# New order tables: value products before gate products, the last scans on the decays themselves, other keep-warm products

## The reference

```python
# layer 0, b = 16 sequences
x = x + attention(q, k, v of layernorm(x), mask_self) @ w_ao + b_ao
x = x + attention(q of layernorm(x), k, v of ctx, mask_cross) @ w_co + b_co
x = x + gelu(layernorm(x) @ w1 + b1) @ w2 + b2
# attention: softmax(q k^T / 4 * mask - 10000 (1 - mask)) v, 16 heads of 16
# layer 1, time mix (states start from ctx)
xn = ln(x); sx = shift(xn) - xn
m = tanh((xn + sx*maa_x) @ maa_w1) -> 5 low-rank mixes @ maa_w2
xw, xk, xv, xr, xg = xn + sx * (stack_i + m_i)
w = exp(-exp(time_decay + tanh(xw @ decay_w1) @ decay_w2))
r, k, v, g = xr@Wr, xk@Wk, xv@Wv, silu(xg@Wg)
s[t+1] = w[t]*s[t] + k[t] v[t]        # a scan along the 128 tokens
o[t] = r[t] . (s[t] + u k[t] v[t])
x = x + (groupnorm(o) * g) @ Wo
# layer 1, channel mix: x = x + sigmoid(xr@Wr') * (relu(xk@Wk')**2 @ Wv')
```

## Time and profile before

| What | Value |
|---|---|
| median of the timed runs | 695.53 us |
| profiled execution, its own time | 695.38 us |
| its span from first to last instruction | 693.6 us |
| around the span | 1.8 us |
| PE busy | 645.6 us (93%) |
| DVE busy | 597.0 us (86%) |
| ACT busy | 570.5 us (82%) |
| POOL busy | 314.9 us (45%) |
| mean granted TensorE clock | 0.985 |
| rounds in the steady part | 37.2 us each |

### The profile page before, as it was taken

The page is one execution under the profiler, slowest core; times in us unless marked ns, Lnnn a source line. Parts: engine busy times, 40 slices in busy tenths (PEclk is TensorE's granted clock), DMA queues, the critical chain, the costliest instruction groups (busy, mean ns, idle before and its releaser), DMA issues.

```text
span 693.6 us, 17394 instructions
## 1 busy us (share of the span) xinstructions
PE 645.6 (93%) x5923; PEld 564.4 (81%) x5923; DVE 597.0 (86%) x1432; ACT 570.5 (82%) x2075; POOL 314.9 (45%) x440
## 2 busy tenths in 40 slices
PE   6778999999999999999999999999999989898876
PEld 5656888788888898898988888888888878787665
DVE  2577668999999999999999999999999996967672
ACT  2579989899999999999999999999999986763311
POOL 1143353555455463626364645455463634441211
PEclk9999999999999999999999999999999999999997
DMA  8920022231405050504122231405050504020200
GB/s 302 329 69 9 1 78 61 62 78 49 98 8 139 1 147 1 144 3 112 35 77 70 62 86 43 104 2 145 1 146 1 139 8 115 24 70 1 69 8 9
DMA packets 53726, 50.45 MB, mean 73 GB/s; under 512 B 6030, under 2 KB 48902, under 8 KB 53254
## 3 DMA queue, kind: packets, MB, share of 16 engines
q1 hardware_dynamic: 53638, 49.34, 25.6%
HBM read 28.62 MB, written 3.93 MB: 47 GB/s over the span
## 4 chain that ended last, share of the span: by engine, by line
PE 71%; ACT 13%; DVE 8%; issue 5%; POOL 2%; DMA 0%; SPq 0%; POOLq 0%; ACTq 0%; DVEq 0%
PE PS_B L542 13%; PE PS_T L637 7%; PE PS_S L542 7%; PE PS_D L549 5%; PE PS_S L618 5%; PE PS_T L645 4%; PE PS_T L549 4%; PE PS_S L549 3%; ACT HG L1240 3%; PE PS_D L783 2%; ACT SC L1199 2%; ACT L1199 2%; PE PS_B L677 2%; PE PS_B L699 2%; ACT PT L1209 2%
## 5 line engine op out<-in xcount | busy, mean ns | idle before, releaser
L1199 ACT ACTIVATE SC<-SC,NMX 128x128 f32<-128x128 f32 x512 | 199.7, 400 | 5.6 <-DVE NMX L934 5.4
L1199 ACT ACTIVATION_READ_ACCUMULATOR SC<-SC,NMX 128x1 f32 x512 | 102.3, 200 | 0.0
L934 DVE TENSOR_REDUCE NMX<-SC 128x4 f32<-128x512 f32 x128 | 85.8, 673 | 0.9 <-POOL SC L1381 0.8
L637 PE MATMUL PS_T<-CST,SC 128*128 128x128 f32 x512 | 79.7, 279 | 5.7 <-ACT SC L1199 2.8
L1209 ACT ACTIVATE PT<-PS_T 128x512 f32<-128x512 f32 x120 | 70.8, 590 | 7.0 <-PE PS_T L637 6.8
L1015 DVE TENSOR_TENSOR_SCAN SS<-W,AJ 128x1024 f32<-128x1024 f32 x32 | 73.1, 2283 | 0.5 <-ACT AJ L1291 0.4
L637 PEld LDWEIGHTS PS_T<-CST,SC 128*128 128x128 f32 x512 | 60.2, 144 | 14.5 <-ACT PT L1209 5.3
L1379 POOL TENSOR_TENSOR SC<-SC,MADD 128x512 f32<-128x512 f32 x48 | 60.2, 1273 | 12.0 <-DVE SC L909 11.9
L542 PE MATMUL PS_B<-MX,W 128*128 128x128 f32 x512 | 62.9, 276 | 0.7 <-ACT KR L1256 0.7
L1381 POOL TENSOR_TENSOR SC<-SC,MADD 128x512 f32<-128x512 f32 x32 | 40.7, 1273 | 48.3 <-DVE SC L909 48.3
L909 DVE TENSOR_TENSOR SC<-PS_S,MASK 128x512 f32<-128x512 f32 x80 | 52.1, 684 | 11.5 <-PE PS_S L618 11.5
(11 more groups left out here) (208 smaller groups left out, 1602.8 us busy)
## 6 DMA issues: line engine op xcount, KB each, us to landing
W<-EW SPq DMA_DIRECT2D x32, 512.0 KB, 4.7
V<-values_by_head SPq DMA_DIRECT2D x28, 512.0 KB, 5.7
W<-in_weights SPq DMA_DIRECT2D x1, 4160.0 KB, 19.6
ENC<-in_enc SPq DMA_DIRECT2D x16, 128.0 KB, 2.4
out<-X SPq DMA_DIRECT2D x16, 128.0 KB, 6.0
X<-in_x SPq DMA_DIRECT2D x1, 1920.0 KB, 15.8
values_by_head<-VC SPq DMA_DIRECT2D x14, 128.0 KB, 1.8
W<-in_weights SPq DMA_DIRECT2D x1, 1280.0 KB, 8.7
```

Source lines behind the costliest of these rows:

```text
L637: last = pe.transpose(PS_T[:, j * T:(j + 1) * T], SC[:, nr(b, a) % 2, g, j, :], ident)
L934: dve.tensor_reduce(NMX[:, nr(b, a) % 2, GH * g:GH * g + GH], SC[:, nr(b, a) % 2, g], AX_X, ALU.max, negate=True)\
L1199: last = act.activation(SC[:, nr(b, a) % 2, g, j, :], SC[:, nr(b, a) % 2, g, j, :], ACT.Exp, bias=NMX[:, nr(b, a) % 2, h:h + 1], accum_out ...
```

## The change

Four things change. First, the value stream moves from the last mixing step to the first and the gate stream to the last; the value product goes to the second bank of `PS_B`, in front of the key and receptance products and with a release of its own (`b_vps`); the gate product keeps its bank and gets `b_gps`. The low-rank columns are brought into a new order by more, smaller DMAs, and the gate's rows lie in a zeroed tile `MG`. Second, for the last sequence each scan is split into 8 scans of 128 elements that read `EW`, without the DMA into `W8`, and the multiplication by r follows each group directly. Third, in the first four attentions the scaled keys are made by VectorE; the turn of the value biases comes behind the first scores, the old output bias is added by a product with the identity, and ScalarE copies the rows out. Fourth, 27 of the keep-warm products around the end are gone (`b_turn` 3 to 0 and 6 to 1, `d_turn` 5 to 0, `d_keyrec` 14 to 0 for the sequences named), and all five order tables are new.

```diff
-MIX_TURNS = [(1, 4), (0, 3), (2,)]
+MIX_TURNS = [(1, 2), (0, 3), (4,)]
-    ('a_query', 1, 1): 2, ('b_turn', 0, 15): 3, ('b_turn', 1, 15): 6, ('d_out', 0, 14): 2, ('d_turn', 0, 14): 5,
-    ('d_keyrec', 0, 14): 14, ('d_val', 0, 14): 2, ('d_own', 0, 15): 2, ('d_read', 0, 15): 2,
+    ('a_query', 1, 1): 2, ('b_turn', 0, 15): 0, ('b_turn', 1, 15): 1, ('d_out', 0, 14): 2, ('d_turn', 0, 14): 0,
+    ('d_keyrec', 0, 14): 0, ('d_val', 0, 14): 2, ('d_own', 0, 15): 2, ('d_read', 0, 15): 2,
...
+    ("b_mlp2", 1, 3), ("a_pv", 0, 1), ("a_val", 0, 0), ("d_keyrec", 0, 5), ("d_keyrec", 1, 5), ("b_turn", 1, 3),
...
             def b_wspread(b, _):
+                if b == B - 1:
+                    return
...
             def b_low1(b, _):
                 pe.wait_ge(b_xx, b + 1)
+                if not later(b):
+                    pe.wait_ge(in_mw, 128)
...
-                        last = pe.matmul(PS_B[:, 0, m * T:(m + 1) * T], w("maa2", 2, C, m * P, (m + 1) * P), MT[:, 0, :],
+                        last = pe.matmul(PS_B[:, 0, m * T:(m + 1) * T], MG[:, m * P:(m + 1) * P], MT[:, 0, :],
...
             def b_decay2(b, _):
                 pe.wait_ge(b_dt, b + 1)
+                pe.wait_ge(b_v, b + 1)
...
             def b_valgate(b, k):
                 if k:
-                    to_channels(PS_B[:, 0, C:2 * C], "g", C, 0, MX[:, 4]).then_inc(b_vgps, 1)
-                else:
+                    pe.wait_ge(b_mx, 3 * b + 3)
                     pe.wait_ge(b_kr, b + 1)
-                    pe.wait_ge(b_mx, 3 * b + 3)
-                    to_channels(PS_B[:, 0, 0:C], "v", C, 0, MX[:, 2])
+                    to_channels(PS_B[:, 0, C:2 * C], "g", C, 0, MX[:, 4]).then_inc(b_gps, 1)
+                else:
+                    pe.wait_ge(b_mx, 3 * b + 1)
+                    pe.wait_ge(b_mix, 3 * b + 2)
+                    to_channels(PS_B[:, 1, C:2 * C], "v", C, 0, MX[:, 2]).then_inc(b_vps, 1)
...
+            def a_key(b, a):
+                if nr(b, a) < FIRST:
+                    dve.wait_ge(a_kps, nr(b, a) + 1)
+                    for par in range(2):
+                        for t in range(CT):
+                            last = dve.tensor_scalar(KP[:, par, t, :], keys[:, t * T:(t + 1) * T],
+                                                     CST[:, K_PAR + par:K_PAR + par + 1], KB[:, a, par, t:t + 1],
+                                                     ALU.mult, ALU.add)
+                    last.then_inc(a_dk, 1)
...
+                if b == B - 1:
+                    for d in range(RS):
+                        last = dve.tensor_tensor_scan(SS[:, t, d, :], EW[:, t, :], AJ[:, t, d, :], 0.0, ALU.mult, ALU.add)
+                    last.then_inc(d_s, 1)
+                    dve.wait_ge(d_s, 2 * b + t + 1)
+                    r = KR[:, 1, t, :].unsqueeze(1).to_broadcast([P, RS, T])
+                    dve.tensor_tensor(SS[:, t], SS[:, t], r, ALU.mult).then_inc(d_rs, 1)
+                    return
...
+                if not later(b, a) and g == 0 and half == 0:
+                    act.wait_ge(set_bv, 1)
+                    act.activation(BVT[:, :, :, :].rearrange("p k t n -> p (k t n)"), PS_D[:, :], ACT.Copy)\
+                        .then_inc(set_bvt, 1)
+                    act.wait_ge(set_bo, 1)
+                    at = ROWS.index("ao"), ROWS.index("co")
+                    for k in range(2):
+                        last = act.activation(ROW[:, at[k], :], PS_D[:, k * C:(k + 1) * C], ACT.Copy)
+                    last.then_inc(set_rows, 1)
```

More of the change, by code:

```diff
@@ L237, in build @@
         a_k = sem("a_k")
+        a_dk = sem("a_dk")
         a_q = sem("a_q")
@@ L602, in a_query @@
                     to_channels(queries, "qkv", 3 * C, 0, A_LT).then_inc(a_qps, 1)
-                    if not later(b):
-                        pe.wait_ge(in_rows, IN_ROWS)
-                        pe.wait_ge(set_dve, 2)
-                        for k in range(2):
-                            last = turn(PS_D[:, k * C:(k + 1) * C], row(f"bv{k}"))
-                        last.then_inc(set_bv, 1)
             def a_scores(b, a):
@@ L622, in a_scores, with a_prob_turn @@
                 if not later(b, a):
+                    pe.wait_ge(in_rows, IN_ROWS)
+                    pe.wait_ge(set_dve, 2)
+                    for k in range(2):
+                        last = turn(PS_D[:, k * C:(k + 1) * C], row(f"bv{k}"))
+                    last.then_inc(set_bv, 1)
+            def a_prob_turn(b, arg):
+                a, g = arg
+                if not later(b, a) and g == 0:
                     pe.wait_ge(in_wa, IN_WA)
                     pe.wait_ge(set_bvt, 1)
-                    to_tokens(PS_D[:, 0:C], "ao", C, 0, BVT[:, 0])
-                    to_tokens(PS_D[:, C:2 * C], "co", C, 0, BVT[:, 1]).then_inc(set_bo, 1)
-            def a_prob_turn(b, arg):
-                a, g = arg
+                    for k, name in enumerate(("ao", "co")):
+                        for kt in range(CT):
+                            pe.matmul(PS_D[:, k * C:(k + 1) * C], BVT[:, k, kt, :], w(name, kt, C, 0, C),
+                                      start=(kt == 0), stop=False)
+                        last = pe.matmul(PS_D[:, k * C:(k + 1) * C], ident, row(name), start=False, stop=True)
+                    last.then_inc(set_bo, 1)
                 warm("a_prob_turn", arg, b)
@@ L692, in b_low2 @@
                     pe.wait_ge(b_mt, b + 1)
-                    if not later(b):
-                        pe.wait_ge(in_mw, 32)
                     for t in range(CT):
@@ L909, in a_mask @@
                 dve.tensor_tensor(masked, PS_S[:, g], over_heads(mask), ALU.mult).then_inc(a_masked, 1)
-                if not later(b, a) and g == 0:
-                    dve.wait_ge(set_bo, 1)
-                    for k, name in enumerate(("ao", "co")):
-                        last = dve.tensor_tensor(row(name), PS_D[:, k * C:(k + 1) * C], row(name), ALU.add)
-                    last.then_inc(set_rows, 1)
             def a_addmask(b, arg):
@@ L1023, in d_rstate @@
             def d_rstate(b, t):
-                if t == 0 or b >= B - LAST:
+                if t == 0 and b < B - 1 or b == B - 2:
                     dve.wait_ge(d_s, 2 * b + t + 1)
@@ L1177, in a_key @@
                 last.then_inc(a_k, 1)
-                if not later(b, a) and par:
-                    act.wait_ge(set_bv, 1)
-                    act.activation(BVT[:, :, :, :].rearrange("p k t n -> p (k t n)"), PS_D[:, :], ACT.Copy)\
-                        .then_inc(set_bvt, 1)
             def a_lessmask(b, _):
```

138 lines of the change are left out of this document (80 added, 58 removed).

## The result

The changed kernel takes 715.75 us (median of three, 714.64 to 716.05) against 695.53: 2.84% slower, with a ratio of 1.0284 and an interval of 1.027 to 1.0298. I had forecast 692.3. The profiled execution (715.75 us, span 714.0) is split at the start of the scores, the products of queries and keys; there is one such group for each of the 32 attentions. The seventh scores start at 107.93 us instead of 104.52, the last at 602.56 instead of 587.09, and from there to the end it is 111.4 us instead of 106.5. So the fill lost 3.4 us, the steady rounds 12.1 and the drain 4.9.

A forecast was written before the change was run, and what follows sets the result against it. PE's own work was taken to bound the steady round (37.01 of 37.21 us), handover chains the fill and drain. Fill -5.1, steady 0, drain +2.0: 695.38 - 3.1 = 692.3 us; its own range 690 to 694.6, overall 687.5 to 697.

The forecast's parts named there:

- the steady term of 0: Steady rounds: extra switch set against decay-stream wait, 0 per round, bounds -0.3 and +0.5, so -3.6 and +6 over 12.
- the extra switch of PE: Each round: a 128-row turn now separates the 32-row low-rank products and scores, 0.15 us dearer per round.
- PE's wait for the decay stream: Steady rounds: PE waits about 0.4 us per round in its weight loads, some 0.2 of it on the chain.
- The warning in my first paragraph: Steady rounds: an idle microsecond badly placed on PE, DVE or ACT would lengthen the round, about 12 times over.
- Rival 1: Steady rounds: PE's turn of B_N waits about 0.5 us for the previous gate, +6, thus 698.3; chance 0.15.
- Fill, -5.1 forecast: First four attentions: earlier scores and exponentials, less ACT key work and shorter waits save 5.1 us; ends -1.2 and -7.2.
- a gain of 0.7 for order and edits together: Fill, first to second scores: first at about 13.6, 1.2 earlier; second at about 33.6 instead of 35.55, -1.9.
- another 3.2 us of the forecast: Fill after the second scores: third near 43.3 (-3.7 in all), then 0.9 and 0.5 more, reaching -5.1.
- +3.1 in the MLP: Drain, sequence 15's MLP: spread, both scans and both r products stand ahead of the next mixes, 3.1 us later than 639.05.
- 3.1 won back: Drain, behind the mixes: the early value product brings sequence 14's residual back to about 654.9, no change.
- +2.0 in the scans: Drain, sequence 15: sixteen short scans, 3.2 us per eight, end CV at 670.8 against 668.83; bounds +0.2 and +4.8.
- the term of 0 for the keep-warm products that went: Drain: removing the warm products put at 0, with -1.5 and +2 (products at the lower clock) as ends.

The follow-up runs named there:

- e1: Changed kernel with VectorE's cross-attention normalise moved ahead of the mask product again; 704.42 us, ratio to the kernel before 1.0114.
- g0: e1 with its first four rounds in the order tables of before, the change's fill edits kept; 704.17 us, ratio 1.012.
- b2: Kernel before with only the change's fill edits (keys on VectorE, bias rows through ScalarE), tables as before; 696.4 us, ratio 1.0019.
- g2: e1 with the old drain order from round 18 on: spread behind the MLP product, scans and r products where they stood; 705.48 us, ratio 1.0139.
- g4: g2 with the gate product ahead of the spread of the values from round 18 on; 708.0 us, ratio 1.0195.
- g3: e1 with the last sequence's scans as two of 1,024 elements on DMA-copied decays instead of sixteen short ones; 704.51 us, ratio 1.0131.
- g1: e1 with all keep-warm products of the kernel before; 705.47 us, ratio 1.0132.
- c1: Changed kernel with e2's two-tensor normalise, nine more keep-warm products in the first attention and g3's long scans; 699.32 us, ratio 1.0042.
- c3: c1 with g2's drain tables from round 18 on; 699.67 us, ratio 1.0047.
- e2: Changed kernel, order kept, cross-attention normalise written with a broadcast second tensor instead of a scalar operand; 701.36 us, ratio 1.0075.

## Why the prediction was wrong

**Steady rounds, 0 forecast, +12.1.** The step that failed is the steady term of 0: it set the extra switch of PE against PE's wait for the decay stream, looked no further, and so put nothing for VectorE. There the normalise, held beside GpSimd, takes 1.50 us instead of 0.41, PE waits 0.84 us for it, and the round is 0.98 us longer. What I did set against each other was right as a sum: in e1 the wait for the decay stream is gone from the list of the weight loads' waits, PE is busy for 0.14 more, and value product, gate product and the new tables together cost next to nothing in a round: e1's 37.24 against 37.21. What I left out was a walk of VectorE's new order beside GpSimd's: which instruction is running on GpSimd when each of them comes up. The warning in my first paragraph, that an idle microsecond in a bad place counts 12 times, was right. Rival 1 had the sign, but neither its mechanism nor its size: no round waits for the gate.

**Fill, -5.1 forecast, +3.4.** First scores came at 14.50 instead of 13.6 (13.61 in the profile of e1, 14.6 to 15.0 in the others with this fill), the first exponential at 20.43 instead of 19.3, second scores at 39.36 instead of 33.6. Three steps failed. First, I carried the earlier start through to the second scores without following the new PE order there: keys and queries of the second attention (16 records, 1.95 us) now stand behind the output product, and ScalarE's first probability copy stands behind twelve exponentials and no longer behind eight, at 25.05 us and not 23.69, with PE idle for it:

```profile
25.67 0.81 PE L662 MATMUL PS_T<-CST,SC 128*128 128x128 f32 x4 [1.94 <-ACT PT L1261]
...
30.97 1.94 PE L670 MATMUL PS_T<-PT,VP 128*32 128x128 f32 x32 [0.78 <-DVE PT L975]
...
36.51 1.95 PE L560 MATMUL PS_S<-A_LT,W 128*128 128x128 f32 x16
39.36 1.15 PE L633 MATMUL PS_S<-KP,QT 32*128 32x256 f32 x16 [0.90 <-DVE QT L934]
```

At a granted clock of 1.00 the step from first to second scores is 21.59 with the new order and 19.5 to 19.6 with the old one (under g0), so the order costs 2.0 us, where I had put a gain of 0.7 for order and edits together. The edits bring nothing, here and in b2.

Second, the clock, which my sum for the fill put at nothing. The probability-times-value product takes 1.94 here and 1.08 at the higher level. The same step took 24.86 in the changed kernel at a clock of 0.79, 3.3 more than at 1.00; before, it was 20.77 at 0.92, 1.2 to 1.3 more. So of the 4.1 us by which the step is longer, about 2.0 are order and about 2.0 clock.

Third, another 3.2 us of the forecast were to come between the second and the seventh scores. That stretch took 68.6 us against 69.0 before, both at a mean clock of 0.98, so 0.4 of it came. Why not more, no run shows. The third scores, for one, stand at 48.83 instead of 43.3 (before at 46.90; the prediction has 46.97).

**Drain, +2.0 forecast (after +3.1 in the MLP, 3.1 won back, +2.0 in the scans), +4.9.** Measured from the last scores in the two profiles:

| Event | before | changed | difference |
|---|---|---|---|
| mixes of sequence 14 | 20.1 | 21.4 | +1.2 |
| B_N, MLP of sequence 15, first | 33.3 | 34.0 | +0.7 |
| B_N, second | 44.8 | 49.2 | +4.5 |
| mixes of sequence 15 | 52.0 | 57.7 | +5.7 |
| D_N of sequence 14 | 70.1 | 74.9 | +4.9 |
| CV of sequence 15 | 81.3 | 86.5 | +5.2 |
| end | 106.5 | 111.4 | +4.9 |

```profile
636.56 0.41 DVE L905 TENSOR_SCALAR B_N<-X,B_MV,B_RS 128x256 f32<-128x256 f32 x1 [0.95 <-POOL B_RS L1404]
...
638.70 0.41 PE L553 MATMUL PS_B<-CST,B_N 128*128 128x128 f32 x2 [1.04 <-issue]
...
645.41 1.95 PE L778 MATMUL PS_S<-VC,SEL 128*128 128x128 f32 x16
...
647.39 1.22 DVE L1042 TENSOR_TENSOR AJ<-PS_S,KR 128x1016 f32<-128x1016 f32 x1 [3.71 <-PE PS_S L778]
...
651.78 0.41 DVE L905 TENSOR_SCALAR B_N<-X,B_MV,B_RS 128x256 f32<-128x256 f32 x1 [0.45 <-POOL B_RS L1404]
...
660.23 1.12 DVE L1021 SCALAR_TENSOR_TENSOR MX<-PS_B,COL,SX 128x128 f32<-128x128 f32 x4
```

The spread in the middle of the MLP was forecast (g2: 2.2 us), and the gap of 3.7 on VectorE as well. Two terms were put too low or too favourably. The turn of `B_N` comes 2.14 us behind it (0.47 before), since the gate's product has to be read out first; I had put 0.35 on that. By the trace its place is the one of rival 1, in the drain only; g4 was meant to test it and did not. And the early value product won back 0.8 between the mixes and `D_N`, not 3.1. There 18.09 us before, at a clock of 0.91, stand against 17.26 at 0.80, with PE's products at the lower level (1.94 for the state read, 1.22 and 1.91 behind it); e1 and g3, with the same order, took 15.97 and 15.90 at 0.89. So about 1.3 us of what is missing go with the clock, and 1 us remains. The scan part was over-sized, +0.3 instead of +2.0. Of the 1.7 between, 1.1 are the scans: a short scan has a pitch of 0.33, not 0.41, and by 2.63 for eight against 2.29 for a long one its fixed part is about 0.04, not the 0.14 that I carried over from products. The rest is that the scans start 3.6 us behind `D_N`, not 4.3:

```profile
681.11 2.63 DVE L1054 TENSOR_TENSOR_SCAN SS<-EW,AJ 128x128 f32<-128x128 f32 x8
683.77 1.23 DVE L1058 TENSOR_TENSOR SS<-SS,KR 128x1024 f32<-128x1024 f32 x1
```

That the direct read of the decays brings nothing fits g3, and the term of 0 for the keep-warm products that went fits g1, within what those runs can tell. The clock alone does not make the drain longer: c1's took 2.9 us more than before at the same mean clock (0.93), c3's 1.5 more at 0.94. How the rest divides between order and clock stays open, since the timed values don't tell c3 and c1 apart.

## What to carry to other kernels

Where a new order moves a one-source VectorE instruction across the one that releases GpSimd, look at what GpSimd does at that moment; the instruction may be held until GpSimd ends. Move it ahead, or write it with a second tensor; here both took the loss away. And in a fill that is bound by latency, walk each engine's new order up to the next hand-over: an earlier start of the first piece says nothing about the second. To compare two orders there, compare stretches that were granted the same clock.

## What the runs showed of the hardware

- A one-source normalise of 256 elements took 1.50 us in place of 0.41 beside a GpSimd add of 1.26, whose end it waited for; the form with two tensors took 0.48, and GpSimd's add 1.53 (e2).
- GpSimd's product of states and r took 3.26 us where VectorE runs the same kind of product beside it, and 2.36 before, where that product stood elsewhere. That the one causes the other was not tried:

```profile
L1476 POOL TENSOR_TENSOR SS<-SS,KR 128x1024 f32<-128x1024 f32 x14 | 45.6, 3260 | 41.8 <-DVE SS L1060 41.8
```

- The same fill order reached the second scores at 36.3 to 36.4 us in two profiles (granted clock 0.77 to 1.00 from 25 to 35 us) and at 39.4 to 40.0 in six (0.50 to 0.71). PE had been idle for 1.9 us ahead of the drop, but also in the two where the clock stayed up. With products in that hole only the earlier time was seen, in three profiles.
